# Four opening steps in four-pass fp32 and undivided steps after them, in a one-core graph layer

## The reference

```python
h = jnp.maximum(_layernorm(x, axis=-1), 0.0)      # x: 8192 x 128
support = jnp.matmul(h, W)                        # W: 128 x 128
out = jnp.matmul(adj, support) + b                # adj: 8192 x 8192, fp32
return x + jax.nn.relu(out)
```

## Time and profile before

| | before |
|---|---|
| median of 3 runs | 726.92 us |
| the runs | 725.5, 727.02, 726.92 us |
| the profiled execution | 725.54 us |
| its span (first to last instruction) | 723.7 us |
| PE / DVE / ACT / POOL busy in the span | 716.3 / 619.8 / 525.4 / 138.1 us |
| moved by DMA | 281.59 MB, mean 389 GB/s |

### The profile page before, as it was taken

One profiled execution on the slowest core, in us unless ns is written; L12 is line 12 of the kernel. 1 busy time (PEld: TensorE's weight loads), 2 busy tenths in 40 slices (PEclk: granted clock), 3 DMA queues, 4 the chain that ended last, 5 costly groups with the idle time before them and its releaser, 6 DMA issues.

```text
span 723.7 us, 7802 instructions
## 1 busy us (share of the span) xinstructions
PE 716.3 (99%) x3130; PEld 588.2 (81%) x3130; DVE 619.8 (86%) x329; ACT 525.4 (73%) x375; POOL 138.1 (19%) x82
## 2 busy tenths in 40 slices
PE   8999999999999999999999999999999999999997
PEld 6788888888888888888888888888888888888885
DVE  7899999899998888888788888888888888888884
ACT  5888888788887767777657777676776667677662
POOL 4347777344555200000000000000000000000000
PEclk9999999999999999999999999999999999999999
DMA  9999999999999999999999999999999999999992
GB/s 356 411 414 415 415 416 416 423 425 421 426 416 383 390 381 408 405 378 398 372 404 364 409 427 410 371 399 369 395 385 393 385 379 395 388 416 380 380 371 74
DMA packets 37908, 281.59 MB, mean 389 GB/s; under 512 B 4336, under 2 KB 4720, under 8 KB 20208
## 3 DMA queue, kind: packets, MB, share of 16 engines
q1 hardware_dynamic: 37440, 280.58, 96.6%
q10 hardware_dynamic: 432, 0.52, 0.2%
HBM read 276.89 MB, written 4.19 MB: 388 GB/s over the span
## 4 chain that ended last, share of the span: by engine, by line
PE 94%; DMA 4%; SPq 1%; ACT 1%; DVE 0%; issue 0%
PE banks L524 93%; DMA raw<-adj 4%; SPq L233 1%; PE banks L550 1%; PE banks L552 1%; PE banks L551 1%; ACT high L356 0%; DVE low L487 0%; DVE sum_low L439 0%; ACT relu_out L341 0%; DVE x_sb L446 0%; ACT sum_high L333 0%; SPq L230 0%
## 5 line engine op out<-in xcount | busy, mean ns | idle before, releaser
L487 DVE TENSOR_TENSOR low<-raw,high 128x3072 fp32r<-128x3072 f32 (+2 forms) x208 | 573.8, 2774 | 90.6 <-PE banks L524 65.0
L356 ACT ACTIVATE high<-raw 128x3072 fp32r<-128x3072 f32 (+2 forms) x208 | 477.8, 2302 | 177.4 <-DMA raw<-adj 172.9
L524 PE MATMUL banks<-high,h_high 128*128 128x512 f32 x1018 | 265.8, 390 | 0.8 <-ACT high L356 0.8
L524 PE MATMUL banks<-high,h_low 128*128 128x512 f32 x1018 | 264.8, 389 | 0.0
L524 PE MATMUL banks<-low,h_high 128*128 128x512 f32 x1018 | 258.9, 389 | 0.0
L524 PEld LDWEIGHTS banks<-high,h_high 128*128 128x128 f32 x1018 | 190.9, 188 | 42.1 <-ACT high L356 1.9
L524 PEld LDWEIGHTS banks<-high,h_low 128*128 128x128 f32 x1018 | 191.1, 188 | 40.1
L524 PEld LDWEIGHTS banks<-low,h_high 128*128 128x128 f32 x1018 | 190.9, 188 | 40.0 <-DVE low L487 0.2
L303 POOL TENSOR_SCALAR z_sb<-x_sb,neg_mean,rstd 128x128 f32<-128x128 f32 x60 | 116.4, 1951 | 1.6
L289 POOL TENSOR_TENSOR rstd<-var_eps,minus_half 128x4 f32<-128x4 f32 (+2 forms) x17 | 21.4, 1261 | 99.0 <-DVE var_eps L396 95.2
L318 ACT ACTIVATE squares<-x_sb,neg_mean 128x128 f32<-128x128 f32 x59 | 22.8, 388 | 6.1 <-DVE neg_mean L390 6.0
(11 more groups left out here) (28 smaller groups left out, 42.6 us busy)
## 6 DMA issues: line engine op xcount, KB each, us to landing
raw<-adj SPq DMA_DIRECT2D x138, 1536.0 KB, 8.9
raw<-adj SPq DMA_DIRECT2D x52, 768.0 KB, 11.6
raw<-adj SPq DMA_DIRECT2D x18, 512.0 KB, 10.2
x_sb<-x_blocks SPq DMA_DIRECT2D x16, 256.0 KB, 8.6
out_blocks<-x_sb SPq DMA_DIRECT2D x16, 256.0 KB, 9.2
x_sb<-x SPq DMA_DIRECT2D x14, 256.0 KB, 11.6
raw<-adj SPq DMA_DIRECT2D x4, 256.0 KB, 5.2
x_sb<-x ACTq DMA_DIRECT2D x1, 256.0 KB, 5.4
```

The lines of the kernel that those rows point to most:

```text
L356: nc.scalar.activation(high[:, t % HIGH_SLOTS, cols], raw[:, t % RAW_SLOTS, cols], ACT.Copy).then_inc(high_ready, 1)
L487: nc.vector.tensor_tensor(low[:, t % LOW_SLOTS, cols], raw[:, t % RAW_SLOTS, cols], high[:, t % HIGH_SLOTS, cols].bitcast(F32), ALU.subtra ...
L524: return nc.tensor.matmul(banks[:, FIRST_BANK[g] + c, :], h[:, (t - FIRST_STEP[g]) * DEPTHS[g] + k, :], tile[:, slot, at:at + BANK], start ...
```

## The change

- Steps 0 to 3 are all done as step 0 was (`FOUR_PASS = 4`): PE multiplies `raw` in plain fp32 with `h_first`, which now has four tiles. ACT and DVE split `adj` from step 4 on only.
- `split_of`: step 0 as before, steps 1 to 3 `[3, 3]`, all later ones whole.
- SP issues all x loads: tile 0 ahead of everything, batch 1 behind the first piece of step 0, batch 2 behind the second; batch 3 ahead of step 2, batch 4 ahead of step 4, batch 5 ahead of step 8, and so on.
- DVE takes the statistics of batches 0 to 3 with bn_stats/bn_aggr; mean, squares and variance of the old kind start with batch 4. ACT's squares of batches 1 and 3 are gone.
- `h_high`/`h_low` of tiles 0 to 3 are made together at step 9, from 128x512 instead of 128x128.
- `rectify` and `rectified_low` come right behind the first piece of their step.
- SP loads steps 4 to 7 when steps 0 to 3 have been multiplied.

```diff
 BATCHES = [(0, 1), (1, 4)] + [(t, t + 4) for t in range(4, TILES, 4)]
+SUMMED_BY_DVE = 4
 EARLY = 4
+FOUR_PASS = 4
...
+    g = group_of(t)
     if t == 0:
         return [1, 1, 2, 2]
-    if t < 6:
-        return [2, 2, 2]
-    if t < 32:
+    if t < FOUR_PASS:
         return [3, 3]
-    g = group_of(t)
     return [1] * WIDTHS[g] if t == LAST else [WIDTHS[g]]
...
+            load_x(0)
             for i in range(len(split_of(0))):
                 load_piece(0, i)
+                if i < 2:
+                    load_x(i + 1)
             for t in range(1, ALL_STEPS):
-                if t in (2, 3):
-                    load_x(t + 1)
-                if t >= 4 and t % 4 == 1 and t // 4 + 4 < len(BATCHES):
-                    load_x(t // 4 + 4)
-                if t == RAW_SLOTS:
-                    sp.wait_ge(products_done, 1)
-                if t > RAW_SLOTS:
+                if t == 2:
+                    load_x(3)
+                if mean_at(t) is not None:
+                    load_x(mean_at(t))
+                if RAW_SLOTS <= t < RAW_SLOTS + FOUR_PASS:
+                    sp.wait_ge(products_done, t - RAW_SLOTS + 1)
+                if t >= RAW_SLOTS + FOUR_PASS:
                     sp.wait_ge(low_ready, halved(t - RAW_SLOTS))
...
-            act.dma_start(x_sb[:, 0, 0:P], x_batches[0]).then_inc(x_first_landed, 16)
-            act.dma_start(x_sb[:, 0, P:BANK], x_batches[1]).then_inc(x_landed[0], 16)
-            act.dma_start(x_sb[:, 1, :], x_batches[2]).then_inc(x_landed[1], 16)
-            square(1, range(1, 4))
-            for t in range(1, ALL_STEPS):
-                if t > HIGH_SLOTS:
+            rectify(2)
+            for t in range(FOUR_PASS, ALL_STEPS):
+                if t >= HIGH_SLOTS + FOUR_PASS:
...
+            statistics(0)
             dve.wait_ge(centre_ready, 1)
             centre(0)
             dve.wait_ge(centred, 1)
             dve.wait_ge(rstd_ready, 1)
...
+            whole(0)
+            statistics(1)
+            statistics(2)
+            for t in range(1, EARLY):
                 centre(t)
...
+            for t in range(1, EARLY):
+                whole(t)
+            statistics(3)
+            rectified_low(2)
+            for t in range(FOUR_PASS, ALL_STEPS):
...
                 if t == 9:
-                    nc.vector.tensor_scalar(h_high[:, 0, :], h_first[:, :], 1.0, None,
+                    nc.vector.tensor_scalar(h_high[:, 0:FOUR_PASS, :], h_first[:, :, :], 1.0, None,
                                             ALU.mult).then_inc(early_high, 1)
...
+            for t in range(FOUR_PASS):
+                pe.wait_ge(h_first_ready, t + 1)
+                for i in range(len(split_of(t))):
+                    pe.wait_ge(raw_landed[t][i], 16)
+                    for c in blocks_of(t, i):
+                        last = nc.tensor.matmul(banks[:, FIRST_BANK[0] + c, :], h_first[:, t, :],
+                                                raw[:, t, c * BANK:(c + 1) * BANK], start=t == 0, stop=False)
+                last.then_inc(products_done, 1)
+
+            for t in range(FOUR_PASS, LAST):
```

More of the change, by code:

```diff
@@ L94, in landed, with batch_at, mean_at, variance_at @@
     return 16 * len([s for s in range(t % RAW_SLOTS, t + 1, RAW_SLOTS) if i < len(split_of(s))])
-def squares_at(t):
-    if t in (2, 3):
[L100 to L120, removed]
+def batch_at(t, phase, ahead):
+    j = t // 4 + ahead
+    return j if t >= FOUR_PASS and t % 4 == phase and j < len(BATCHES) else None
+def mean_at(t):
+    return batch_at(t, 0, 3)
+def variance_at(t):
+    return batch_at(t, 2, 3) if t >= 4 else None
+def rectified_at(t):
+    return batch_at(t, 2, 2)
+def squares_at(t):
+    j = batch_at(t, t % 4, 3) if t >= 4 and t % 4 in (1, 2) else None
+    if j is None:
+        return None
+    at = BATCHES[j][0] + (t % 4 - 1) * 2
+    return j, range(at, at + 2)
 def x_slot(j):
@@ L164, in gnn_layer @@
         warm = sb("warm", [P, P])
-        h_first = sb("h_first", [P, P])
-        stats = sb("stats", [P, 5, 6])
-        moments = sb("moments", [P, 5, 2])
+        h_first = sb("h_first", [P, FOUR_PASS, P])
+        stats = sb("stats", [P, BATCHES[SUMMED_BY_DVE - 1][1], 6])
+        moments = sb("moments", [P, BATCHES[SUMMED_BY_DVE - 1][1], 2])
         W_sb = sb("W_sb", [P, P])
@@ L357, in _ @@
                                          ACT.Copy).then_inc(high_ready, 1)
+                    if i == 0 and rectified_at(t) is not None:
+                        rectify(rectified_at(t))
                 if squares_at(t) is not None:
                     square(*squares_at(t))
-                if rectified_at(t) is not None:
-                    rectify(rectified_at(t))
                 if t == 9:
@@ L394, in variance @@
                 first, end = BATCHES[j]
-                dve.wait_ge(squared, end - 1 if j == 1 else end - 5)
+                dve.wait_ge(squared, end - BATCHES[SUMMED_BY_DVE][0])
                 nc.vector.tensor_scalar(var_eps[:, first:end], sum_squares[:, first:end], 1.0 / P, EPS,
                                         ALU.mult, ALU.add).then_inc(var_ready, 1)
[L399 to L408, removed]
+            def statistics(j):
+                first, end = BATCHES[j]
+                if j == 0:
+                    dve.wait_ge(x_first_landed, 16)
+                else:
+                    dve.wait_ge(x_landed[x_slot(j)], x_landed_count(j))
+                for t in range(first, end):
+                    cols = slice(t % 4 * P, t % 4 * P + P)
+                    nc.vector.bn_stats(stats[:, t, :], x_sb[:, x_slot(j), cols]).then_inc(stats_ready, 1)
+                dve.wait_ge(stats_ready, end)
+                for t in range(first, end):
+                    nc.vector.bn_aggr(moments[:, t, :], stats[:, t, :]).then_inc(moments_ready, 1)
+                dve.wait_ge(moments_ready, end)
+                nc.vector.tensor_scalar(var_eps[:, first:end], moments[:, first:end, 1], EPS, None,
                                         ALU.add).then_inc(var_ready, 1)
-                nc.vector.tensor_scalar(neg_mean[:, first:end], moments[:, here, 0], -1.0, None,
+                nc.vector.tensor_scalar(neg_mean[:, first:end], moments[:, first:end, 0], -1.0, None,
                                         ALU.mult).then_inc(centre_ready, 1)
@@ L489, in _ @@
                                             ALU.subtract).then_inc(low_ready, 1)
+                    if i == 0 and rectified_at(t) is not None:
+                        rectified_low(rectified_at(t))
                 if mean_at(t) is not None:
@@ L558, in _ @@
                 nc.tensor.matmul(banks[:, PSUM_BANKS - 1, 0:P], warm[:, :], warm[:, :], start=True, stop=True)
-            pe.wait_ge(h_first_ready, 1)
-            for i in range(len(split_of(0))):
-                pe.wait_ge(raw_landed[0][i], 16)
-                for c in blocks_of(0, i):
-                    last = nc.tensor.matmul(banks[:, FIRST_BANK[0] + c, :], h_first[:, :],
-                                            raw[:, 0, c * BANK:(c + 1) * BANK], start=True, stop=False)
-            last.then_inc(products_done, 1)
-            for t in range(1, LAST):
+            for t in range(FOUR_PASS):
[7 more added lines that the diff above has]
+            for t in range(FOUR_PASS, LAST):
                 g = group_of(t)
@@ L589, in _ @@
                             last = product(t, c, k, h_low, high, t % HIGH_SLOTS)
-                last.then_inc(high_used, 1)
-                for i in pieces:
+                    if i == pieces[-1]:
+                        last.then_inc(high_used, 1)
                     pe.wait_ge(low_ready, halved(t, i))
```

77 lines of the change are left out of this document (22 added, 55 removed).

## The result

The change makes the kernel slower: 732.39 us (median of 4 runs, 731.97 to 732.85) against 726.37 (725.5 to 727.02), a ratio of 1.0087 with a 95% interval of 1.0075 to 1.0100, +6.0 us (the ratio stands for 6.3). The forecast was +2.0 us and 728.9, with a range of 726.8 to 730.8. The profiled executions, 731.98 and 725.54, lie 6.4 apart.

A forecast was written before the change was run, and what follows sets the result against it. PE alone was taken to set the end from step 6 on; +1.1 us for PE's path, +0.6 for step 4's undivided chain and +0.3 for an instruction block made +2.0, 728.9 us, range 726.8 to 730.8.

The forecast's parts named there:

- What bounds before: From 36.04 us on PE alone, without waits, sets the end; earlier waits for ACT and its transfers cost 1.35 us.
- PE's +1.1: PE's path to step 6: +3.2 us for three fp32 steps, -1.4 for waits gone, -0.7 for the earlier start.
- S6: The time PE starts step 6, freed of the wait inside it: 34.68 us before, forecast 36.4, or 36.6 to 37.1.
- The 6.3 us from landing to `low`: Undivided step 4: ACT's copy and DVE's subtraction together need 6.34 us from the transfer's landing until `low` is ready.
- The landing of step 4 at 24.5: Step 4's last piece, before at 24.8 us, was to land at 24.5, bounds 23.9 and 25.0.
- The +0.6 of the sum: Delay before step 6 because the undivided chain of copy and subtraction is not ready for step 4: +0.6 us.
- What costs nothing: The moved work on ACT, DVE and POOL, SP's later loads and batch 5's later load were to cost 0 us.
- Rival 3: DVE becomes the bound through steps 7 to 12, +3.5 to +5 us, 731; chance 0.12.
- The block of instructions: An instruction fetch moves to step 7 or 8, making landings 1.1 to 1.4 us late; +0 to +0.7, taken +0.3.
- Rival 4: PE's clock rises later in step 0, lengthening PE's path by up to 3.1 us, 731.2; chance 0.08.
- Rivals 2 and 5: 2: PE alone, earlier landings, +1.1 us, 728.0, chance 0.2. 5: lagging landings of steps 5 and 6 vanish, 726.6, chance 0.1.

The follow-up runs named there:

- before_whole: The kernel before with steps from 4 on undivided, this part of the change alone; 729.22 us, ratio 1.0051.
- order_back: The changed kernel with squares ahead of rectify on ACT and the variance ahead of rectified_low on DVE, as before the change; 729.56 us, ratio 1.0054.
- rectify_later: The changed kernel with rectify and rectified_low behind the fourth step of four instead of the third; 729.97 us, ratio 1.0063.
- x_on_act: The changed kernel with x batches 0, 1 and 2 issued by ACT again instead of SP; 731.93 us, ratio 1.0087.
- the second look at before: The kernel before, unchanged, profiled a second time; that execution took 725.4 us.
- the two versions with pieces: Changed kernel, steps 4 to 31 in two pieces, x batches 0 to 2 on ACT (1.0005); LayerNorm part, old pieces, four fp32 steps (1.0026).
- four_fp32_alone: The changed kernel with the old pieces, x batches 0 to 2 on ACT and the old variance order, four fp32 steps kept; 727.82 us, ratio 1.0026.

## Why the prediction was wrong

- **What bounds before: right. PE's +1.1: right in its price per step, 0.6 short in its start.** PE alone set the end once it ran without waits, and the fp32 records are 0.43 apart. But the fp32 stretch ends at 28.2 instead of my 27.6 (28.2 + 2 x 4.09 = 36.4, +1.7 instead of +1.1). The start came 1.2 earlier (4.6, tile 0 landed at 2.5), but PE then waited 1.71 and 0.77 for pieces 1 and 2 of step 0, which I hadn't counted: x now stood ahead of them. With pieces behind the fp32 steps S6 is 35.9, +1.2.
- **The 6.3 us from landing to `low`: right (26.8 to 33.0). The landing of step 4 at 24.5: the mis-sized term.** It landed at 26.8, outside my bounds of 23.9 to 25.0. I took the same bytes at the same time as before and one profile's 24.8 as a fixed number; it moves by 1.2 to 1.8 from run to run, and the changed kernel's step 0 landed 2.3 later than in that profile. ACT's copy from 26.82, PE's `low` wait to 33.02: S6 = 38.6 instead of 36.4. The +0.6 of the sum is +2.2. The waits at step 4 were 1.24 and 0.38, where I had forecast 0.3 to 1. Before, pieces made a late landing harmless; undivided, it goes straight to step 6, as the table of seven profiles shows. In before_whole step 4 landed on time, ACT took it at 25.0, and undivided it still cost 3.0 us by step 6, some 0.6 of it clock (last section): there PE was free early and stood waiting, so the chain's length is the loss and not the landing.
- **"What costs nothing": the failed step, 2.7 us.** I costed moving `rectified_low` ahead of the variance at nothing, and looked at POOL only for batch 2. Behind the variance there then stands a whole subtraction, and POOL's power takes 4.04 instead of 1.37. The page before had the sign: POOL's z averages 1.95 us over the kernel, where a tile of batch 2 can take 0.45. order_back takes 2.4 us away without changing DVE's or POOL's work. Rival 3 had the place (steps 7 to 12, then 15) but named DVE as the bound; rectify_later rules that out.
- **The block of instructions: as forecast in place, not in effect.** It came at 35 to 37 us, and S7 to S12 stood at 38.6 to 38.7 throughout. In x_on_act and rectify_later, waits that add up to 1.6 to 1.7 us appear in steps 8 to 10, with step 8 landed at 43.5 and 44.0 instead of 42.4; that the block is behind that is argued, not shown. I had also priced it from one profile: in the second look at before the block comes at 28 to 30, and step 5 lands 4.5 behind step 4, the time that its bytes need, and not 5.9.
- **Rival 4 (clock)** is visible as spread, 0.5 us in S6 between the two versions with pieces, and 1.7 us of the fp32 stretch in rectify_later. There S6 did not move, against the rival's own words that nothing would hide it: the undivided chain did. **Rivals 2 and 5** fell.

The account: +1.7 (PE's fp32 path with its waits), +2.2 (step 4 undivided and landed late), +2.7 (POOL, at step 15), 6.6 us. These are places along one profile, not prices of parts: the fp32 steps alone cost 1.7 in four_fp32_alone, but undivided steps alone 3.7 in before_whole, and the two overlap ahead of step 6. How late the first transfers landed was in part chance of the execution. Either error alone would have left the time in the range of 726.8 to 730.8: 732.4 less 2.2 is 730.2, and less 2.7 it is 729.7. By that reckoning, an estimate from the terms above, it took both.

## What to carry to other kernels

In these traces a POOL instruction issued while a two-input DVE subtraction runs is held until that one ends (4.04 us for a power of 1.01), so the instruction that stands *between* a DVE result and the next long subtraction decides when POOL's answer comes; when moving work, write down for POOL's chain which DVE gap each of its instructions uses. Pieces buy insensitivity: with them a transfer may land a microsecond late unseen, without them the sum of copy and subtraction stands behind it. And one profile's landing time is one draw; a sum that has no slack there needs a second profile.

## What the runs showed of the hardware

POOL's power over 128x4 took 1.0 us beside an idle DVE, 1.38 beside a 0.69 us scalar_tensor_tensor and 4.04 beside a 3.35 us tensor_tensor; z of 128x128 took 0.45 alone, 2.6 to 3.8 behind one subtraction and 5.8 behind two. Beside a tensor_reduce, which has one input, it took 0.44. The Trainium skill has it (SBUF — State Buffer, section SBUF: two separate sides): DVE and GpSimd share one port pair, held for a whole instruction by whichever starts first, also by a DVE operation with two SBUF inputs against a GpSimd one that reads SBUF. The traces agree for POOL's side of it; I had not weighed it. The other way round they agree in part: a subtraction that began while a z ran took 3.6 (at 77.11 in the changed kernel), but the power ran its last 0.87 us (61.54 to 62.41) beside one that took the usual 3.35.

A wait can cost more than itself. In before_whole PE waited 2.93 us for step 4, and the granted clock fell to 0.56 on average of the next 3.6 us, nine matmuls where sixteen would fit; most are 0.43 apart instead of 0.227, the level of 1.2 GHz (timeline, then windows with PEclk third from last):

```profile
27.79 2.56 PE L522 MATMUL banks<-high,h_high 128*128 128x512 f32 x6 [2.93 <-ACT high L354]
```

```profile
24.50:27.80 3.30, 0.37 (x3) 0.01 (x1) 0.00 (x0) 2.76 (x1) 1.98 (x5) 1.00 1.07 444
27.80:31.40 3.60, 3.60 (x9) 2.81 (x10) 3.56 (x2) 2.07 (x1) 0.00 (x0) 0.56 1.03 437
```

`low` of step 4 was there at 31.20 and PE asked for it at 32.23, so the echo was 1.0 us long. I estimate that about 0.6 of it reached the end, as step 6's copy was done only at 37.06 and PE started the step at 37.67. In the changed kernel the waits of 1.24 and 1.43 us had no such echo: the granted clock behind both is 1.00.
